# Attention part of a one-block transformer tower: probabilities fetched a step later, joining ended a batch sooner, mask and row maximum in one VectorE operation per head

## The reference, cut to what matters

```python
h = s4d_kernel(log_dt, x, B, inv_A_real, A_imag)            # (32, 128, 1024)
h = concatenate([cls_tok, h], axis=1)                        # 32 batches of 129 rows
# attention: 32 query heads of 32, 8 key/value heads, 4 query heads to each
xn = layernorm(h)
q, k, v = xn @ Wq.T, xn @ Wk.T, xn @ Wv.T                    # then rotary positions on q and k
scores = q @ k.T / sqrt(32);  scores = where(causal, scores, lowest)
attn = softmax(scores);       ctx = attn @ v
h = h + ctx @ Wo.T
h = h + fake_quant(layernorm(h)) @ fake_quant(w).T + b
```

## Time and profile before

| | |
|---|---|
| median of three runs | 1458.92 us |
| profiled execution | 1462.95 us, of which the span of the core is 1461.2 us |
| granted TensorE clock, mean | 0.985 |
| PE busy | 1399.9 us (96% of the span) |
| DVE busy | 1167.3 us (80%) |
| POOL busy | 919.3 us (63%) |
| ACT busy | 729.4 us (50%) |
| mean DMA rate | 175 GB/s |

### The profile page before, as it was taken

How to read it: one execution, slowest core, us unless ns; L and a number is a source line. 1 busy time by engine, 2 the same in 40 slices (tenths; PEclk the granted TensorE clock), 3 DMA queues, 4 the chain that set the end, 5 groups by cost and what they waited for, 6 DMA issues and landing times.

```text
span 1461.2 us, 34142 instructions
## 1 busy us (share of the span) xinstructions
PE 1399.9 (96%) x10403; PEld 1107.9 (76%) x10434; DVE 1167.3 (80%) x2285; ACT 729.4 (50%) x2675; POOL 919.3 (63%) x958
## 2 busy tenths in 40 slices
PE   5999898999999999999999999789999999999997
PEld 3999767777788788887888888567677777777775
DVE  8988678999999999999999999586865655556565
ACT  7997566666767767777776777551100000000000
POOL 6896156676776767677676767345655556565553
PEclk8999999999999999999999999889999999999999
DMA  9456676777777777777777777857534444343432
GB/s 242 117 140 155 188 156 153 204 197 204 217 199 218 196 212 207 207 211 207 217 198 214 200 206 197 263 178 224 149 118 133 122 129 134 117 136 115 142 104 75
DMA packets 264217, 255.72 MB, mean 175 GB/s; under 512 B 72321, under 2 KB 201346, under 8 KB 264162
## 3 DMA queue, kind: packets, MB, share of 16 engines
q1 hardware_dynamic: 254210, 233.60, 57.6%
q10 hardware_dynamic: 9952, 21.43, 4.7%
HBM read 138.26 MB, written 106.97 MB: 168 GB/s over the span
## 4 chain that ended last, share of the span: by engine, by line
PE 71%; DVE 11%; DMA 5%; POOL 5%; issue 3%; SPq 3%; ACT 1%; DVEq 0%; ACTq 0%; POOLq 0%
PE att_ps L1117 28%; PE ffn_o L1799 23%; PE ffn_y L1903 7%; DMA p_blocks<-pB 4%; PE att_ps L1162 4%; PE att_ps L1176 4%; POOL yb L357 3%; SPq L886 2%; POOL yb L363 2%; PE att_ps L1151 2%; PE mix_ps L446 1%; PE att_ps L1141 1%; DVE sm L1423 1%; DVE pB L1416 1%; DVE m L642 1%
## 5 line engine op out<-in xcount | busy, mean ns | idle before, releaser
L1252 ACT ACTIVATE pr<-sm,ml 128x128 f32<-128x128 f32 x1024 | 399.1, 393 | 134.8 <-DVE ml L1432 132.9
L996 POOL TENSOR_TENSOR pr<-pr,ri 128x512 f32<-128x512 f32 x256 | 266.3, 1040 | 234.1 <-DVE ri L1439 233.8
L1117 PE MATMUL att_ps<-w_hi,xT_hi 128*128 128x512 f32 x776 | 315.6, 407 | 4.3 <-DVE xT_lo L1380 3.5
L1117 PE MATMUL att_ps<-w_lo,xT_hi 128*128 128x512 f32 x776 | 315.8, 407 | 0.0
L1117 PE MATMUL att_ps<-w_hi,xT_lo 128*128 128x512 f32 x776 | 307.2, 396 | 0.0
L1799 PE MATMUL ffn_o<-wo_hi,cT_hi 128*128 128x512 f32 x528 | 212.4, 402 | 1.9 <-ACT wo_hi L1837 1.4
L1416 DVE STREAM_TRANSPOSE pB<-pr 128x512 f32<-128x512 f32 x256 | 178.1, 696 | 42.6 <-DMA p_blocks<-pB 37.7
L1853 ACT CAST cT_hi<-ctx_in 128x512 fp32r<-128x512 f32 x64 | 36.3, 616 | 348.1 <-PE ffn_o L1799 348.1
L1799 PE MATMUL ffn_o<-wo_hi,cT_lo 128*128 128x512 f32 x528 | 206.2, 390 | 0.0
L1799 PE MATMUL ffn_o<-wo_lo,cT_hi 128*128 128x512 f32 x528 | 205.9, 390 | 0.0
L1252 ACT ACTIVATION_READ_ACCUMULATOR pr<-sm,ml 128x1 f32 x1024 | 193.4, 189 | 0.0
(11 more groups left out here) (219 smaller groups left out, 2333.7 us busy)
## 6 DMA issues: line engine op xcount, KB each, us to landing
pT<-p_blocks SPq DMA_DIRECT2D x256, 256.0 KB, 2.9
p_blocks<-pB SPq DMA_DIRECT2D x512, 64.0 KB
h_rows<-ho SPq DMA_DIRECT2D x64, 256.0 KB, 4.4
ctx_turned<-ctxo SPq DMA_DIRECT2D x64, 256.0 KB, 3.0
h_in<-h_rows SPq DMA_DIRECT2D x32, 512.0 KB, 3.8
out_dram<-yo SPq DMA_DIRECT2D x32, 512.0 KB, 2.6
ctx_in<-ctx_turned SPq DMA_DIRECT2D x30, 512.0 KB, 3.2
hbuf<-h_rows ACTq DMA_DIRECT2D x29, 512.0 KB, 5.0
```

The costliest lines, as they stand in the source:

```text
L996: G.tensor_tensor(pr[:, g % 4], pr[:, g % 4], ri[:, g % 2, :].unsqueeze(2).to_broadcast([P, GQ, P]), ALU.mult).then_inc(p_ready, 1)
L1117: mm = nc.tensor.matmul(bank[:], x_part[:, t[1], e, tok:tok + P], w_part[blk][:, e, :], start=(r == 0), stop=(r == EC * 3 - 1))
L1252: a = nc.scalar.activation(pr[:, g % 4, q, :], sm[:, g % 2, q, :], ACT.Exp, bias=ml[:, b[1], 0, h:h + 1], accum_out=ml[:, b[1], 1, h:h + 1])
```

## The change

Three edits stand in one diff.

First, `whole_p` goes from lag 6 to lag 7, and the two waits on `weighed` in `part_p` go from g = 2 and 6 to g = 3 and 7.

Second, `weighed_late` is false from body NB-2 = 30 on, and the lag of 5 for `whole_p` holds for the last three batches (29 to 31) where it held for two.

Third, `mask` does both pieces of DVE's work: for each of the four query heads one `tensor_tensor_reduce` writes the negated masked score (128x128) and the minimum of its row, so four operations stand in the place of the two; `row_maximum` and its semaphore go, and a `memset` of one column comes ahead of the four. `masked` is signalled behind the last of the four and is also what ACT waits for. The exponential takes `scale=-1.0` to undo the sign.

```diff
     def weighed_late(t):
-        return not (fixed(t) and number(t) >= NB - 1)
+        return not (fixed(t) and number(t) >= NB - 2)
...
             for q in range(4):
-                if q == 3 and g == 2:
+                if q == 3 and g == 3:
                     at_least(sp, weighed, 2 * number(b) - 1)
-                if q == 3 and g == 6:
+                if q == 3 and g == 7:
                     at_least(sp, weighed, 2 * number(b))
...
-                d, g = group_at(t, s, 6)
-                if exists(d, NB) and not (fixed(d) and number(d) >= NB - 2):
+                d, g = group_at(t, s, 7)
+                if exists(d, NB) and not (fixed(d) and number(d) >= NB - 3):
                     whole_p(d, g)
                 d, g = group_at(t, s, 5)
-                if exists(d, NB) and fixed(d) and number(d) >= NB - 2:
+                if exists(d, NB) and fixed(d) and number(d) >= NB - 3:
                     whole_p(d, g)
...
-            act.wait_ge(negmax_ready, n + 1)
+            act.wait_ge(masked, n + 1)
...
-                a = nc.scalar.activation(pr[:, g % 4, q, :], sm[:, g % 2, q, :], ACT.Exp,
+                a = nc.scalar.activation(pr[:, g % 4, q, :], sm[:, g % 2, q, :], ACT.Exp, scale=-1.0,
...
-            V.tensor_tensor(sm[:, g % 2], S_BANK[g % 4][:].rearrange("p (q k) -> p q k", q=GQ),
-                            cst[:, C_MASK:C_MASK + P].unsqueeze(1).to_broadcast([P, GQ, P]),
-                            ALU.add).then_inc(masked, 1)
-
-        def row_maximum(b, g):
-            n = STEPS * number(b) + g
             if g == 0 and (not fixed(b) or number(b) >= 2):
                 v.wait_ge(ml_stored[b[1]], 16 * b[0])
-            v.wait_ge(masked, n + 1)
-            V.tensor_reduce(ml[:, b[1], 0, heads_of(g)], sm[:, g % 2], AX.X, ALU.max, negate=True
-                            ).then_inc(negmax_ready, 1)
+            V.memset(gates[:, g:g + 1], 0.0)
+            for q in range(GQ):
+                h = 16 * (g // 4) + 4 * q + g % 4
+                last = V.tensor_tensor_reduce(sm[:, g % 2, q], S_BANK[g % 4][:, q * P:(q + 1) * P],
+                                              cst[:, C_MASK:C_MASK + P], -1.0, 3.0e38, ALU.add, ALU.min,
+                                              ml[:, b[1], 0, h:h + 1])
+            last.then_inc(masked, 1)
```

More of the change, by code:

```diff
@@ L689, in attention_stage @@
     pB, v_new = sbuf["pB"], sbuf["v_new"]
-    ml, ri, st, mv, ve, rstd, gate, wmax, wsc, winv = small_sb
+    ml, ri, st, mv, ve, rstd, gate, wmax, wsc, winv, gates = small_sb
     ps = [psum[f"att_ps{i}"] for i in range(8)]
@@ L745, in attention_stage @@
     masked = shared["masked"]
-    negmax_ready = sem("negmax_ready")
     exp_done = sem("exp_done")
@@ L1465, in body @@
                     mask(d, g)
-                    row_maximum(d, g)
                 if s == 7 and x_steps(n)[1] is None and has_rows(n):
@@ L2141, in program @@
         att_small = (sb("ml", (2, 2, HEADS)), sb("ri", (2, GQ)), sb("st", (2, 6)), sb("mv", (2,)), sb("ve", (1,)),
-                     sb("rstd", (1,)), sb("gate", (1,)), sb("wmax", (EC,)), sb("wsc", (EC,)), sb("winv", (EC,)))
+                     sb("rstd", (1,)), sb("gate", (1,)), sb("wmax", (EC,)), sb("wsc", (EC,)), sb("winv", (EC,)), sb("gates", (HKV,)))
         ffn_small = (sb("ffn_st", (2, 6)), sb("ffn_mv", (2,)), sb("ffn_ve", (1,)), sb("ffn_rstd", (1,)),
```

## The result

The changed kernel took 1470.98 us (median of 11 runs, 1458.08 to 1473.37), the kernel before 1458.92 us in the same sitting. The ratio is 1.0074, 95% interval 1.0054 to 1.0095: some 11 us slower by the ratio, 12 by the medians. The forecast of no change was wrong. The 11 times lie in two bunches: three from 1458.1 to 1464.4 and eight from 1469.5 to 1473.4. The profiled execution is the fastest of them (1458.08 us, span 1456.3), so its trace shows what the change does when little goes wrong. The loss has to be read from other executions.

The account below looks back on a forecast made before the run. PE bounds the middle, VectorE nearly touching. Start -0.5, middle 0, later fetch 0, joining sooner +2.8 - 0.7 - 2.0 sum to -0.4 us: 1458.5 us against 1458.92, range 1449 to 1484 us.

Parts of the forecast that it names:

- Group cost: Steady bodies of attention: VectorE's time per mask group, taken as 1.18 us for 1.29 before, between 0.86 and 1.86 us.
- rival A: Steady bodies of attention: VectorE becomes the bound, slower by 24 us (1483 us), at most 99 us (1558 us); chance 0.22.
- Its sign: Middle of attention: PE waiting for `masked` there would show that VectorE had become the bound.
- The middle: Steady bodies of attention: PE still sets the pace, the fourth mask being ready 0.6 us early; change 0.
- break-even: Fourth mask of a half body: PE is held up only if a group costs over 1.33 us, or 1.54 in the other half.
- The start: Start of attention, 225 to 345 us: VectorE's saving against the later release, taken as -0.5 us, from -4 to +3.
- Rival B: Both ends of attention: start -4 us and body 31's writes -6 us win, -8 us in all, 1451 us; chance 0.25 with lesser gains.
- The fetch a step later: Middle of attention: fetch and its wait moved a step add no instruction and free nothing; cost 0.
- Joining sooner: Bodies 30 and 31: PE waits +2.8 us for a fetch in body 30, then -0.7 and -2 us in body 31.
- The return: Body 31: the wait at 923 us goes, -0.7 us; store and fetch leave the crowded stretch, -2 us (0 to -6).
- Rival C: Ends of attention: body 30's 2.8 us wait paid, body 31's queue still full, start loses up to 1 us; +4 us, 1463 us; chance 0.11.

## Why the prediction was wrong, step by step

- **Group cost.** Taken 1.18 us, measured 0.85, the lower bound. The hand-out of the minimum, priced at 0.08 us per head from the reciprocal's rows, lies wholly beside the next head. It is a row of its own, as the prediction cited from the Trainium skill ("VectorE: DVE Perf Modes", "Two Vector instructions with no wait between them") while no row of before showed it. The rule cited for rival A's upper end has an exception in its own section ("The DRAIN you can't avoid"), that an operation which is not held starts earlier; heads 0.21 us apart, each shown with 0.28 us, agree with the exception. Rival A, VectorE as the bound at 24 us or more, did not come: VectorE has more room than before. Its sign did come, PE waiting for `masked` in the middle, but from another cause.
- **The middle.** This is the step that failed, a wait put at nothing: "With 1.18 us the first is ready at 645.34, 0.6 us early: the middle stays PE's, change 0." The break-even moved the four masks up as if VectorE's starts were set by VectorE alone, and "POOL and the transposition are no earlier for it" was taken as harmless. In fact the transposition waits for writes whose landing depends on when another queue puts 512 KB on the same engines. In the profiled execution of the mask edit alone PE lost 0.2 to 1.0 us in most bodies, 10.0 us from 350 to 890 us; this execution took 12.1 us more than the median of the kernel before. Of the changed kernel itself no execution of the upper bunch (1469 us and more) was profiled; the slower of its two traces (1465.79 us) lost 3.7 us in the same way, up to 560 us. I had read VectorE's lateness and SP's queue, not the load on ACT's, which has no wait of its own in any view of the kernel before.
- **What the trace of before did show.** Bodies kept writes 1.7 to 2.2 us ahead of the load. With VectorE's order as in the change, PE was late only at spacings up to 1.24 us, and not in every such body; the changed kernel in its good rhythm has 1.4 us and more. In the trace that holds both, the lag of a body repeats in the next until it dies out at 590 us. Shown is that the load's place among the writes decides, for an order in which a transposition stands ahead of the masks; with the masks first, 0.1 to 0.2 us did no harm. That the thinner margin is how the start's unevenness comes to stay was only argued, and by which property the mask edit thins it is open.
- **The start.** Taken -0.5 us. PE's busy time from 203 to 348 us rose by 1.3 us in the changed kernel as it stood, one trace each. With the load out of the way it rose from 135.44 us in the kernel before to 139.98 in the mask edit with the moved load: 4.5 us, the optimistic end. Rival B's view of the start was right once the load stood elsewhere; with the old operations the moved load brought 1.0 us of it.
- **The fetch a step later.** 0 in the middle is right. Its cost lies at the end, and where depends on the joining edit: without it a wait of 4.19 to 4.59 us in body 31, with it the wait in body 30 (2.39 us with the moved load), which mask, joining and moved load with the lag of 6 do not have.
- **Joining sooner.** The wait of 2.8 us in body 30 came as 2.14 us in the changed kernel. It takes both edits, the lag as much as the joining: the joining edit alone has no wait for a fetch in that body and is no change (0.9996). The return came as forecast, in size at least: the wait at 923 us is gone, PE's idle time from 935 to 960 us fell from 11.5 to 8.7 us (taken: -0.7 and -2.0), and the longest landing of writes on the chain there is 5.8 us.
- **Rival C** (1463 us) had the sign, not the mechanism: the ends cost 2 to 4 us by the lag, and the rest of the loss is not at the ends. The range, 1449 to 1484, held the time by luck: its upper part was there for rival A, which did not happen.

## What to carry to other kernels

A wait that is absent from the profile may be absent by a margin of half a microsecond. When an edit shifts two engines against each other, look at every pair of transfers that are near neighbours in time on different queues, and measure their distance body by body before and after. Where a kernel's times fall in two bunches, profile until both are seen, because the trace of the lucky run does not show the loss; and a large load with a body of slack belongs away from small writes that a busy engine waits for.

## What the runs showed of the hardware

- A VectorE operation that adds and takes a row minimum in one costs 0.21 us per 128x128 head from start to start, nearly as a plain add of that shape (0.20); the read of its accumulator is shown with 0.08 us and overlaps the next one. The Trainium skill ("VectorE: DVE Perf Modes", "The TRN2 errata") gives an estimated 0.26 us for the shape; the rows have 0.28 to 0.29 us for one operation as shown and 0.21 us from start to start, so the estimate fits neither.
- Four writes of 32 to 64 KB landed within 1.3 to 1.7 us of their last issue where a load of 512 KB on the other queue was issued 1.7 us or more behind their start, and 3.2 to 5.1 us after it where the load came 0.6 to 1.3 us behind their start, with the same bytes moved overall.
- One more VectorE instruction per group, 16 in a pass of the loop, took the mask edit from 1467 to 1510 us (ratios 1.0045 and 1.0339, two sittings), and five more per group did no worse (1.0349). Why so small an addition costs so much is argued above, not measured.
